# A 3025-point Fourier transform split into 121 by 25 points in place of 55 by 55

## The chip, the core and the metric

The kernel runs on one core of one Trainium2 chip, as one program. The metric is the device time of one execution in microseconds (us), as the median of several runs. The core's engines are TensorE (PE; its weight loads are listed apart as PEld), VectorE (DVE), ScalarE (ACT) and GpSimd (POOL); SyncE (SP) issues most of the transfers.

## The reference

Two layers on a batch of 64 images of 55 x 55 pixels with 96 channels. Layer 0 is a depthwise convolution with 9 x 9 taps, three pixels apart, and a gate. Layer 1 treats the 3025 pixels of an image as tokens: a normalisation, a linear layer to 192 channels with a relu, a Fourier transform along the tokens, a gate on the spectrum, the inverse transform, a linear layer back to 96 channels; then a feed-forward layer with fp8 operands.

```python
def _L1_attn_ref(x, w1, ..., bn2_mean, bn2_var):
    h = jnp.einsum('bnc,hc->bnh', x, w1)
    h = jax.nn.relu(_bn(h, bn1_gamma, bn1_beta, bn1_mean, bn1_var))
    X = jnp.fft.fft(h, axis=1, norm='ortho')
    rd = jnp.diagonal(r)
    idg = jnp.diagonal(i)
    xr = jax.nn.relu(X.real * rd - X.imag * idg + rb)
    xi = jax.nn.relu(X.imag * rd + X.real * idg + ib)
    y = jnp.fft.ifft(xr + 1j * xi, axis=1, norm='ortho').real.astype(jnp.float32)
    o = jnp.einsum('bnh,ch->bnc', y, w2)
    return _bn(o, bn2_gamma, bn2_beta, bn2_mean, bn2_var)

x = _L0_conv_ref(x, L0_conv_raw_kernel, L0_conv_bias)
t = _to_tokens(x)                                  # 64 x 3025 x 96
t = t + _L1_attn_ref(_ln_t(t), ...)
t = t + _L1_ffn_ref(_ln_t(t), L1_ffn_W1, L1_ffn_b1, L1_ffn_W2, L1_ffn_b2)
```

## The kernel before

`conv_stage` computes layer 0 and writes it to `x1` in device memory. `mixer_stage` then sets up constants and runs layer 1, an image (called a batch below) at a time. Its instructions are written out by hand for each engine, in `part(i, ...)`, which `run_all` calls for i = 0 to 66, most of them in a loop. A part works on four batches at once: the forward transform's first half of batch i, its second half, gate, mixing and first inverse half of batch i-1, the last inverse half of batch i-2, and the feed-forward layer of batch i-3. Semaphores tie the engines together.

The transform of 3025 = 55 x 55 points is done in two steps of 55. Tokens lie on 110 partitions, the 55 image rows twice (`NP`), with 28 and 27 token columns side by side (`J` = 28 columns in all, one half padded). The spectrum of a real signal is symmetric, so 28 first frequencies (`K1`) suffice.

A part has two halves.
- First half, loop over h: `turn` transposes the tokens (`tok`), `widen` makes 192 channels of a token column, ACT's `relu` writes `hid`, `rows` is the transform along the partitions (`fa`), DVE's `rows_out` copies it to `arow`, and SP stores that to `a_d`. In between, in eight tiles (`TILE_AT`), `columns` does the second transform of the batch before with weights from `acol`, two tiles of 7 frequencies each at a time in PSUM; ACT's `gate_in`, DVE's `gate` and `join` and POOL gate the spectrum into `spec`. DVE also normalises `xn2` for the feed-forward layer. `acol` is loaded from `a_d`, with the axes exchanged by the address pattern.
- Second half, loop over seven chunks c of four token columns (`JC`): `mix` (two matmuls a frequency, spectrum to 96 channels), `up` (fp8, 384 channels of 440 token slots), `inverse` (second transform backwards, weights from `mixed`), `inverse_rows` (first transform backwards, from `grow`), `down` (fp8, back to 96 channels, weights from `hq`). ACT copies each from PSUM; DVE adds a bias and casts to `hq`, adds the residual into `t2` and takes statistics (`stats`, `variance`) of the coming tokens between the first two chunks; POOL adds the last bias and the output. SP stores `mixed` to `g_d`, loads `grow` from it and `t_res` from `x1`, and stores the output.

`up(c+1)` reuses PSUM that ACT has to empty, and `down(c)` waits for the cast of chunk c (`hq_ready`), so PE, ACT and DVE pass each chunk around.

Of the kernel before, what the change touches and what calls it, by code (L numbers as in the profile page):

```python
# [114 lines left out]


def transform_constants():

    n = np.arange(R)
    k1 = np.arange(K1)  # L120
    ang = 2 * np.pi * np.outer(n, k1) / R
    fwd = np.concatenate([np.cos(ang), -np.sin(ang[:, 1:])], axis=1)
    inv = np.concatenate([np.cos(ang), -np.sin(ang[:, 1:])], axis=1).T
    fa = np.zeros((NP, NP))
    ia = np.zeros((NP, NP))
    for p in range(2):
        fa[p * R:(p + 1) * R, p * R:(p + 1) * R] = fwd
        ia[p * R:(p + 1) * R, p * R:(p + 1) * R] = inv
    k = k1[:, None] + R * n[None, :]
    th = 2 * np.pi * ((n[:, None, None] * k[None]) % (R * R)) / (R * R)  # L130
# [1 line left out]
    fb = np.zeros((NP, K1, NP))
    fb[:R, :, :R] = co
    fb[R:, :, :R] = si
    fb[:R, :, R:] = -si
    fb[R:, :, R:] = co
    w = np.where(k1 == 0, 0.5, 1.0)[None, :, None]
    ib = np.zeros((NP, K1, NP))
    ct, st = (v.transpose(2, 1, 0) * w for v in (co, si))
    ib[:R, :, :R] = ct  # L140
    ib[:R, :, R:] = st
    ib[R:, :, :R] = -st
    ib[R:, :, R:] = ct
    out = {"c_fa": fa, "c_fb": fb, "c_ib": ib, "c_ia": ia, "c_id": np.eye(128)}
# [132 lines left out]
def mixer_stage(nc, x1, p, a_d, g_d, out):  # L277
    with ExitStack() as ctx:
# [22 lines left out]
        b2q = sb("b2q", [NP, C], F16)  # L301


        t_in = sb("t_in", [NP, J, C])
        tok = sb("tok", [NP, J, C + 1])
        xnt = [sb(f"xnt{s}", [C + 1, JC, NP]) for s in range(2)]
        hid = [sb(f"hid{s}", [NP, 2, H]) for s in range(2)]
        arow = [sb(f"arow{s}", [NP, JC, H]) for s in range(AR)]
        acol = sb("acol", [NP, K1, H])
        spec = sb("spec", [HH + 1, 2, K1, NP])  # L310
# [811 lines left out]
```

## Time and profile before

| | us |
|---|---|
| median of 3 runs | 6499.09 |
| lowest, highest | 6497.29, 6509.12 |
| the profiled execution | 6508.48 |
| its span, first to last instruction | 6506.7 |
| PE busy | 5635.0 (87%) |
| DVE busy | 4653.9 (72%) |
| ACT busy | 3317.6 (51%) |
| POOL busy | 2185.0 (34%) |

The convolution takes the first 1050 us or so, the mixer the rest. A table of stretches gives for each the busy time of every engine, the granted TensorE clock (PEclk, 1.00 is full speed), the busy share of the 16 DMA engines and GB/s. A row of a timeline merges like instructions that follow each other: its start, its time to the end of the last, the count as x14, and in brackets the idle time ahead of it with what ended it. An f32 matmul leaves two records, so x14 are 7 matmuls. The end of a matmul is modelled, so its price is read from start to start.

### The profile page before, as it was taken

The numbers are of one execution on the slowest core, as the hardware profiler recorded it, in microseconds if no ns is written. First come the engines' busy times: TensorE is split into PE (matmuls) and PEld (weight loads), VectorE is DVE, ScalarE is ACT, GpSimd is POOL, SyncE is SP. The second block draws the span as 40 slices with busy tenths as digits, with TensorE's granted clock in tenths as the row PEclk, the third lists the DMA queues.
The fourth block names the chain that finished last, engine by engine and source line by source line (L and its number), as shares of the span: only waits on it lengthen the run. The fifth ranks groups of instructions, "written<-read, shape, count | busy, mean of one in ns | idle before, by whom it ended". The sixth has DMA issues, their size and how long they took to land. (4 is left out here: it accounts for less than half of the span.)

```text
span 6506.7 us, 139542 instructions
## 1 busy us (share of the span) xinstructions
PE 5635.0 (87%) x43722; PEld 4751.2 (73%) x43722; DVE 4653.9 (72%) x13238; ACT 3317.6 (51%) x6661; POOL 2185.0 (34%) x1924
## 2 busy tenths in 40 slices
PE   8899994698888888888888888888888888888886
PEld 8898994577777777777777777777777777777775
DVE  4555664367777777777777777777777777777776
ACT  0000000356666666666666666666666666666664
POOL 0000000134444444444444444444444444444443
PEclk9999997789999999999999999999999999999996
DMA  6666664455555555555555555555555555555552
GB/s 219 181 179 189 178 184 113 101 128 132 128 129 129 129 129 128 128 127 128 127 128 128 128 128 128 128 128 128 128 129 129 129 129 128 128 129 129 129 127 60
DMA packets 877318, 875.70 MB, mean 135 GB/s; under 512 B 433439, under 2 KB 805535, under 8 KB 868895
## 3 DMA queue, kind: packets, MB, share of 16 engines
q1 hardware_dynamic: 806005, 784.39, 48.8%
q10 hardware_dynamic: 71174, 89.35, 4.5%
q8 instruction: 100, 1.64, 0.1%
q14 instruction: 39, 0.32, 0.0%
HBM read 497.81 MB, written 375.77 MB: 134 GB/s over the span
## 5 line engine op out<-in xcount | busy, mean ns | idle before, releaser
L646 POOL TENSOR_TENSOR spec<-spec,gc 96x385 f32<-96x385 f32 x512 | 485.7, 949 | 2506.6 <-DVE spec L837 2506.6
L655 POOL TENSOR_TENSOR z<-z,b2q 110x384 f16<-110x384 f16 x448 | 558.7, 1247 | 1622.7 <-ACT z L753 1622.7
L978 PEld LDWEIGHTS ps<-fb,acol 110*96 110x96 f32 (+1 forms) x7168 | 737.9, 164 | 358.9 <-DVE gv L841 230.6
L978 PE MATMUL ps<-fb,acol 110*96 110x110 f32 (+1 forms) x7168 | 817.9, 264 | 122.3 <-DVE gv L841 110.7
L686 ACT ACTIVATE hid<-ps,rstd 110x192 f32<-110x192 f32 x1792 | 660.0, 427 | 487.8 <-PE ps L948 487.2
L958 PE MATMUL ps<-hid,fa 110*110 110x384 f32 x1792 | 754.8, 503 | 165.7 <-ACT hid L686 83.0
L1005 PE MATMUL ps<-w2t,spec 97*110 97x96 f32 x3584 | 742.6, 293 | 13.7 <-DVE spec L848 6.2
L948 PE MATMUL ps<-w1t,xnt 97*110 97x192 f32 x3584 | 734.1, 327 | 0.6 <-ACT xnt L678 0.6
L245 DVE SCALAR_TENSOR_TENSOR xout<-cps,xin 114x351 f32<-114x351 f32 (+3 forms) x512 | 402.4, 786 | 443.4 <-PE cps L272 443.4
L1007 PE MATMUL ps<-w2t,spec 96*110 96x96 f32 x3584 | 718.4, 286 | 0.0
L827 DVE COPY arow<-ps 110x384 f32<-110x384 f32 x896 | 494.6, 552 | 288.0 <-PE ps L958 218.1
L857 DVE TENSOR_TENSOR t<-ps,t_res 110x384 f32<-110x384 f32 x448 | 248.9, 556 | 629.9 <-PE ps L928 488.0
L649 POOL TENSOR_SCALAR gv<-gv 96x385 f32<-96x385 f32 x512 | 657.3, 1284 | 110.7 <-DVE gv L841 110.7
L1064 PEld LDWEIGHTS ps<-w2q,hq 128*110 128x110 fp8e5 x5376 | 397.5, 154 | 406.1 <-issue 378.4
L268 PE MATMUL cps<-xin,toep 114*114 114x117 f32 (+3 forms) x3072 | 615.3, 283 | 87.2 <-DMA xin<-in_x 72.3
L948 PEld LDWEIGHTS ps<-w1t,xnt 97*110 97x110 f32 x3584 | 562.2, 175 | 97.9 <-ACT xnt L678 0.9
L746 ACT ACTIVATE y<-ps 128x1320 f16<-128x1320 f32 x448 | 569.1, 1270 | 106.4 <-PE ps L1048 80.5
L1064 PE MATMUL ps<-w2q,hq 128*110 128x96 fp8e5 x5376 | 415.3, 236 | 233.2 <-issue 225.9
L1005 PEld LDWEIGHTS ps<-w2t,spec 97*110 97x110 f32 x3584 | 583.4, 206 | 35.5 <-issue 29.2
L272 PE MATMUL cps<-xin,toep 114*114 114x96 f32 (+1 forms) x3072 | 570.9, 268 | 0.0
L1007 PEld LDWEIGHTS ps<-w2t,spec 96*110 96x110 f32 x3584 | 569.2, 203 | 0.0
L477 ACT ACT_TABLE_LOAD x1 | 1.3, 1283 | 1079.9 <-PEq L150 1079.9
(103 smaller groups left out, 11789.9 us busy)
## 6 DMA issues: line engine op xcount, KB each, us to landing
a_d<-arow SPq DMA_DIRECT2D x896, 165.0 KB
acol<-a_d SPq DMA_DIRECT2D x64, 1155.0 KB
acol<-a_d SPq DMA_DIRECT2D x64, 1113.8 KB
out<-o_sb SPq DMA_DIRECT2D x832, 82.5 KB
xin<-in_x SPq DMA_DIRECT2D x256, 211.5 KB, 5.4
g_d<-mixed SPq DMA_DIRECT2D x64, 660.0 KB
x_d<-xout ACTq DMA_DIRECT2D x144, 263.2 KB
tok<-x_d SPq DMA_DIRECT2D x64, 577.5 KB
```

The costliest lines, as they stand in the source:

```text
L268: nc.tensor.matmul(o[0:GP, :], toep[0:GP, ch, GP:2 * GP], xs[:, pad:pad + cols], start=True, stop=False)
L272: last = nc.tensor.matmul(o[0:GP, 0:cols - step + pad], toep[0:GP, ch, 0:GP], xs[:, step + pad:], start=False, stop=True)
L649: nc.gpsimd.tensor_scalar(gv[t % 2][:, :, :], gv[t % 2][:, :, :], 0.0, None, ALU.max).then_inc(v_cut, 1)
L655: nc.gpsimd.tensor_tensor(z16[c % 2][:, :, :], z16[c % 2][:, :, :], b2, ALU.add).then_inc(z_biased, 1)
L686: last = nc.scalar.activation(hid[h % 2][:, j, :], ps[0:NP, 5 + h % 2, j * H:(j + 1) * H], ACT.Relu, scale=rstd[0][:, 2 * h + j:2 * h + j ...
L746: nc.scalar.activation(y16[c % 2][:, :, :], ps[:, 4:4 + FM, 0:TOK], ACT.Copy).then_inc(y16_ready, 1)
L948: last = nc.tensor.matmul(ps[0:NP, 5 + h % 2, j * H:(j + 1) * H], xnt[c % 2][:, 2 * (h % 2) + j, :], w1t[:, :], start=True, stop=True)
L958: nc.tensor.matmul(ps[0:NP, 7, 0:2 * H], fa[:, :], hid[h % 2][:, :, :].rearrange("p j h -> p (j h)"), start=True, stop=True).then_inc(a_do ...
L978: last = nc.tensor.matmul(ps[0:HH, 2 - 2 * (t % 2) + n // 4, 128 * (n % 4):128 * (n % 4) + NP], acol[0:kk, k1, hf * HH:(hf + 1) * HH], fb[ ...
L1005: nc.tensor.matmul(o, spec[0:HH + 1, 0, k1, :], w2t[0:HH + 1, 0, :], start=True, stop=False)
L1007: last = nc.tensor.matmul(o, spec[0:HH, 1, k1, :], w2t[0:HH, 1, :], start=False, stop=True)
L1064: last = nc.tensor.matmul(ps[0:NP, 7, C * j:C * (j + 1)], hq[c % 2][:, m, j * NP:(j + 1) * NP], w2q[:, m, :], start=(m == 0), stop=(m == F ...
```

## The change

The tokens now lie on 121 partitions with 25 columns each, which holds 3025 tokens with no padding. The transform is one of 121 points along the partitions and one of 25 along the columns. 61 first frequencies suffice; they are taken in pairs, 31 of them (`PAIRS_K`), each pair with its real and imaginary parts and 25 second frequencies on 100 partitions or columns (`Q`). In `a_d`, `g_d`, `grow` and `arow` the first frequencies are padded to 32 pairs, 128 rows (`M`).

| | before | after |
|---|---|---|
| partitions x token columns | 110 x 28 | 121 x 25 |
| chunks of token columns | 4 x 7 | 4, 4, 4, 4, 3, 3, 3 |
| frequencies in `columns` tiles | 7 x 8 | 8 x 6, 7 x 2 |
| frequencies in `mix` and `inverse` groups | 4 x 7 | 5, 5, 5, 4, 4, 4, 4 |
| size of a `columns` matmul (partitions, weights, moving) | 110, 96, 110 (two of 55) | 100, 96, 100 |
| size of a `mix` matmul | 97 or 96, 110, 96 | 97 or 96, 100, 96 |
| DMAs of a part (`tok`, `t_res`, `grow`, `a_d`, `acol`, `g_d`, `out`) | 2, 2, 4, 14, 2, 2, 14 | 1, 1, 2, 7, 2, 2, 7 |

The load of `acol` now reads runs of 31 x 192 values in two pieces, the store of `arow` writes runs of 192. The unused `t_in` is gone, and with it three memsets of the set-up (`tok`, `t_res`, `grow`); one of 96 values on 100 partitions comes in. The core of the diff:

```diff
-K1 = R // 2 + 1
-J = 28
-NP = 2 * R
+U = 121
+S = 25
+KH = U // 2 + 1
+PAIRS_K = (KH + 1) // 2
+SLOTS = PAIRS_K + 1
+M = 4 * SLOTS
+Q = 4 * S
+CHUNK = (0, 4, 8, 12, 16, 19, 22, 25)
+MIXED = (0, 5, 10, 15, 19, 23, 27, 31)
+GROUP = (0, 8, 16, 24, 31)
+PART = (0, 7, 13, 19, 25)
...
-                nc.vector.memset(tok[:, :, 0:C], 0.0)
-                for v in (t_res, grow):
-                    nc.vector.memset(v[:, :, :], 0.0)
+                nc.vector.memset(mixed[:, PAIRS_K, :], 0.0)
...
-                        for pp in range(2):
-                            sp.dma_start(a_d[i, :, pp * J + JC * c:pp * J + JC * (c + 1), :],
-                                         arow[c % AR][pp * R:(pp + 1) * R, :, :]).then_inc(a_stored[c % AR], 16)
+                        sp.dma_start(a_d[i, c0:c1, :, :].rearrange("s m h -> m s h"),
+                                     arow[c % AR][:, 0:c1 - c0, :]).then_inc(a_stored[c % AR], 16)
...
-                    for ri in range(2):
-                        src = a_d[i, ri * K1:ri * K1 + K1 - ri, 0:R, :].rearrange("k n h -> n k h")
-                        sp.dma_start(acol[ri * R:(ri + 1) * R, ri:K1, :], src).then_inc(acol_in, 16)
+                    src = a_d[i].rearrange("s (r p) h -> (s r) p h", p=SLOTS)
+                    for p0, p1 in ((0, 16), (16, PAIRS_K)):
+                        sp.dma_start(acol[:, p0:p1, :], src[:, p0:p1, :]).then_inc(acol_in, 16)
...
-                    for n in range(KC):
-                        k1 = g * KC + n
-                        kk = R if k1 == 0 else NP
+                    for n in range(pairs):
                         last = nc.tensor.matmul(
-                            ps[0:HH, 2 - 2 * (t % 2) + n // 4, 128 * (n % 4):128 * (n % 4) + NP],
-                            acol[0:kk, k1, hf * HH:(hf + 1) * HH], fb[0:kk, k1, :], start=True, stop=True)
+                            ps[0:HH, 2 - 2 * (t % 2) + n // 4, 128 * (n % 4):128 * (n % 4) + Q],
+                            acol[:, p0 + n, hf * HH:(hf + 1) * HH], fb[:, p0 + n, :], start=True, stop=True)
```

How the order on PE changes at the end of a part's first half, before (`columns` is L978, `widen` L948, `turn` L939, `rows` L958; the numbers are the output's partitions x columns and the count):

```order
L978 MATMUL ps<-fb,acol 96x110 x7
L948 MATMUL ps<-w1t,xnt 110x192 x2
L939 MATMUL ps<-ident,tok 97x110 x4
L958 MATMUL ps<-hid,fa 110x384
L948 MATMUL ps<-w1t,xnt 110x192 x2
L958 MATMUL ps<-hid,fa 110x384
L978 MATMUL ps<-fb,acol 96x110 x7
```

and in the changed kernel (`columns` is L1007, `widen` L978, `turn` L969, `rows` L989):

```order
L1007 MATMUL ps<-fb,acol 96x100 x7
L978 MATMUL ps<-w1t,xnt 121x192 x2
L969 MATMUL ps<-ident,tok 97x121 x3
L989 MATMUL ps<-hid,fa 128x192
L978 MATMUL ps<-w1t,xnt 121x192
L989 MATMUL ps<-hid,fa 128x384
L1007 MATMUL ps<-fb,acol 96x100 x7
```

The order of the groups stays; every second `widen` and `rows` here has one token column in place of two.

The end of a part's second half on PE, before (`up` L1048, `inverse` L1036, `inverse_rows` L928, `down` L1064):

```order
L1048 MATMUL ps<-xq,w1q 128x440 x3
L1036 MATMUL ps<-mixed,ib 110x96 x4
L928 MATMUL ps<-grow,ia 110x384
L1064 MATMUL ps<-w2q,hq 110x96 x12
L1036 MATMUL ps<-mixed,ib 110x96 x4
L928 MATMUL ps<-grow,ia 110x384
L1064 MATMUL ps<-w2q,hq 110x96 x12
L928 MATMUL ps<-grow,ia 110x384 x2
```

and in the changed kernel (L1078, L1065, L958, L1094):

```order
L1078 MATMUL ps<-xq,w1q 128x363 x3
L1065 MATMUL ps<-mixed,ib 100x96 x4
L958 MATMUL ps<-grow,ia 121x384
L1094 MATMUL ps<-w2q,hq 121x96 x9
L1065 MATMUL ps<-mixed,ib 100x96 x4
L958 MATMUL ps<-grow,ia 121x288
L1094 MATMUL ps<-w2q,hq 121x96 x9
L958 MATMUL ps<-grow,ia 121x288 x2
```

Nothing moves here either; the last three chunks have three token columns.

DVE between the first two casts to `hq`, ahead of the second `down`, before:

```order
L901 CAST hq<-y 128x1320
L774 BN_STATS bn<-tok 110x6 x7
L786 TENSOR_TENSOR mean<-bn 110x28
L787 TENSOR_TENSOR diff<-bn 110x28
L788 TENSOR_TENSOR var<-bn 110x28
L789 TENSOR_SCALAR mean<-mean 110x28
L790 SCALAR_TENSOR_TENSOR sq<-diff 110x28
L792 TENSOR_TENSOR var<-var,sq 110x28
L793 TENSOR_SCALAR sq<-var 110x28
L895 TENSOR_SCALAR y<-y,b1q 128x440 x3
L901 CAST hq<-y 128x1320
```

and in the changed kernel:

```order
L930 CAST hq<-y 128x1452
L800 BN_STATS bn<-tok 121x6 x6
L812 TENSOR_TENSOR mean<-bn 121x25
L813 TENSOR_TENSOR diff<-bn 121x25
L814 TENSOR_TENSOR var<-bn 121x25
L815 TENSOR_SCALAR mean<-mean 121x25
L816 SCALAR_TENSOR_TENSOR sq<-diff 121x25
L818 TENSOR_TENSOR var<-var,sq 121x25
L819 TENSOR_SCALAR sq<-var 121x25
L924 TENSOR_SCALAR y<-y,b1q 128x484 x3
L930 CAST hq<-y 128x1452
```

One `bn_stats` less, and adds and casts of 484 slots in place of 440. From the fifth chunk on the cast is `128x3x363`, three rows of 363, since its buffers are 484 wide.

## Rows read from the trace of the kernel before

**Rows 1.** The page's head.

```profile
span 6506.7 us, 139542 instructions
```

**Rows 2.** Timeline of PE: the first `columns` of three batches; start us, us, what.

```profile
1439.86 1.35 PE L978 MATMUL ps<-fb,acol 55*96 55x110 f32 x10
...
1517.69 1.73 PE L978 MATMUL ps<-fb,acol 55*96 55x110 f32 x14
...
5040.47 0.79 PE L978 MATMUL ps<-fb,acol 55*96 55x110 f32 x4
```

**Rows 3.** Timeline of PE: waits ahead of the second and the last `down`.

```profile
1494.10 0.78 PE L1064 MATMUL ps<-w2q,hq 128*110 128x96 fp8e5 x12 [1.81 <-issue]
...
3046.70 1.32 PE L1064 MATMUL ps<-w2q,hq 128*110 128x96 fp8e5 x12 [1.81 <-issue]
...
3071.95 0.78 PE L1064 MATMUL ps<-w2q,hq 128*110 128x96 fp8e5 x12 [1.46 <-issue]
```

**Rows 4.** Stretches: length, busy of PE, PEld, DVE, ACT, POOL; PEclk, DMA share, GB/s.

```profile
1493.00:1498.00 5.00, 3.90 (x41) 3.60 (x42) 2.44 (x6) 2.25 (x5) 1.91 (x2) 1.00 0.78 160
...
3045.00:3050.00 5.00, 3.30 (x24) 3.33 (x25) 3.04 (x8) 1.42 (x4) 1.21 (x2) 0.66 0.78 161
3050.00:3055.00 5.00, 5.00 (x22) 3.75 (x22) 0.00 (x0) 2.25 (x3) 0.61 (x1) 0.50 0.65 156
3055.00:3060.00 5.00, 5.00 (x43) 4.47 (x42) 4.31 (x11) 2.28 (x4) 2.44 (x2) 0.81 0.00 0
```

**Rows 5.** Timeline of PE in the convolution.

```profile
600.50 0.33 PE L270 MATMUL cps<-xin,toep 114*76 114x96 f32 x2
600.67 0.36 PE L272 MATMUL cps<-xin,toep 114*114 114x96 f32 x2
600.87 0.38 PE L268 MATMUL cps<-xin,toep 114*114 114x117 f32 x2
```

**Rows 6.** Timeline of PE: one chunk of the second half.

```profile
3060.52 0.40 PE L1005 MATMUL ps<-w2t,spec 97*110 97x96 f32 x2
...
3062.11 0.72 PE L1048 MATMUL ps<-xq,w1q 96*128 96x440 fp8e5 x3
3062.67 0.92 PE L1036 MATMUL ps<-mixed,ib 110*110 110x96 f32 x8
3063.43 0.82 PE L928 MATMUL ps<-grow,ia 110*110 110x384 f32 x2
3064.09 0.77 PE L1064 MATMUL ps<-w2q,hq 128*110 128x96 fp8e5 x12
3064.69 0.40 PE L1005 MATMUL ps<-w2t,spec 97*110 97x96 f32 x2
```

**Rows 7.** Timeline of PE: groups of the first half, later and first of a batch.

```profile
3009.93 1.49 PE L978 MATMUL ps<-fb,acol 110*96 110x110 f32 x14
3011.26 0.82 PE L948 MATMUL ps<-w1t,xnt 97*110 97x192 f32 x4
3011.91 0.81 PE L958 MATMUL ps<-hid,fa 110*110 110x384 f32 x2
...
3078.42 1.73 PE L978 MATMUL ps<-fb,acol 55*96 55x110 f32 x14
3079.98 0.82 PE L948 MATMUL ps<-w1t,xnt 97*110 97x192 f32 x4
```

**Rows 8.** Timeline of DVE: statistics and casts.

```profile
3041.02 1.21 DVE L774 BATCH_NORM_STATS2 bn<-tok 110x6 f32<-110x96 f32 x7
...
3045.75 0.85 DVE L901 CAST hq<-y 128x1320 fp8e5<-128x1320 f16 x1
...
3070.52 1.33 DVE L901 CAST hq<-y 128x1320 fp8e5<-128x1320 f16 x1
```

**Rows 9.** Groups by form: line, operation, shapes, count | busy us, mean ns | idle before.

```profile
L817 DVE TENSOR_SCALAR xn<-t,mean,rstd 110x96 f32<-110x96 f32 x1792 | 509.1, 368 | 0.1
...
L469 DVE MEMSET grow<- 110x2688 f32 x1 | 2.3, 2298 | 0.5 <-issue 0.5
```

More of the change, by code:

```diff
@@ L110, with half @@
 ROOT_C = 3
-QJ = J // 4
-PAIRS = NC * 2
 TILE_AT = (0, 2, 4, 6, 7, 9, 10, 12)
-TOK = JC * NP
+def half(h):
+    c0, c1 = CHUNK[h // 2], CHUNK[h // 2 + 1]
+    return (c0, c0 + 2) if h % 2 == 0 else (c0 + 2, c1)
 def transform_constants():
[L119 to L130, printed above, removed]
-    co, si = np.cos(th) / R, np.sin(th) / R
[L132 to L144, printed above, removed]
@@ L300, in mixer_stage @@
         b1q = sb("b1q", [128, FM])
[L301 to L310, printed above, removed]
-        gc = [sb(f"gc{s}", [HH, KC, R]) for s in range(2)]
-        gq = [sb(f"gq{s}", [HH, KC, R]) for s in range(2)]
@@ L313, in mixer_stage @@
[L313 to L319 removed]
+        b2q = sb("b2q", [U, C], F16)
+        tok = sb("tok", [U, S, C + 1])
+        xnt = [sb(f"xnt{s}", [C + 1, JC, U]) for s in range(2)]
+        hid = [sb(f"hid{s}", [U, 2, H]) for s in range(2)]
+        arow = [sb(f"arow{s}", [M, JC, H]) for s in range(AR)]
@@ new lines, in mixer_stage @@
+        acol = sb("acol", [Q, PAIRS_K, H])
+        spec = sb("spec", [HH + 1, 2, PAIRS_K, Q])
+        gc = [sb(f"gc{s}", [HH, KC, Q // 2]) for s in range(2)]
+        gq = [sb(f"gq{s}", [HH, KC, Q // 2]) for s in range(2)]
+        gv = [sb(f"gv{s}", [HH, KC, Q // 2]) for s in range(2)]
+        mixed = sb("mixed", [Q, SLOTS, C])
+        grow = sb("grow", [M, S, C])
+        t_res = sb("t_res", [U, S, C])
+        t2 = sb("t2", [U, S, C])
+        xn2 = sb("xn2", [U, S, C])
+        xq = sb("xq", [C, N], F8)
@@ L331, in mixer_stage @@
+        rstd = [sb(f"rstd{s}", [U, S]) for s in range(2)]
         ps = ctx.enter_context(nc.psum_tensor("ps", [128, 8, 512], F32))
@@ L688, in relu @@
+                    act.wait_ge(a_done, i * HALVES + max(h - 1, 0))
+                    s0, s1 = half(h)
+                    for j in range(s1 - s0):
+                        last = nc.scalar.activation(hid[h % 2][:, j, :], ps[0:U, 5 + h % 2, j * H:(j + 1) * H],
+                                                    ACT.Relu, scale=rstd[0][:, s0 + j:s0 + j + 1])
                     last.then_inc(hid_ready, 1)
                 def gate_in(t):
-                    g, hf = t // 2, t % 2
+                    p0, p1, _, hf = group(t)
@@ L709, in part @@
                     turn_out(0)
-                for h in range(PAIRS + 2):
-                    if first and 1 <= h <= PAIRS:
+                for h in range(HALVES + 2):
+                    if first and 1 <= h <= HALVES:
                         relu(h - 1)
```

323 lines of the change are left out of this document (177 added, 146 removed).

## The prediction

> **What bounds the kernel now.** The profiled execution spans 6506.7 us [rows 1] and took 6508.48; the median of the runs shown is 6499.09, 9.4 below it. The convolution stage is not touched, so everything turns on the mixer. Its batches are alike: the first `columns` of the batch starts at 1517.69 and, 43 batches later, at 5040.47 [rows 2], which is 3522.78 / 43 = 81.925 us a batch. 58 batches of the trace have that length.
>
> Read the waits of TensorE (PE) next. PE is busy in almost all of a batch, and its longest waits are two: 1.81 us before the second `down` (it waits for VectorE (DVE), which does statistics and a variance between the two casts `hq`), and 1.46 us before the last `down` [rows 3]. Then read the granted clock. After the 1.81 us wait it is 0.66, 0.50, 0.81 in three stretches of 5 us [rows 4]: full speed is 2.4 GHz, 0.50 is 1.2 GHz, and the three make 2 x 5 x (0.34 + 0.50 + 0.19) = 10.3 us at half speed. This happens once a batch. One batch shows what it costs: in the one before 1517.69 the same wait (1494.10, also 1.81 us) is followed by a clock of 1.00 (the stretch from 1493), and that batch lasts 1517.69 - 1439.86 = 77.83 us [rows 2, 3, 4]. So **a batch is 77.83 us of work and waits, and 4.10 us for one drop of the clock.** After the 1.46 us wait the clock never falls in the batches of that length.
>
> **The price of a matmul.** In the convolution a matmul with 76 weight columns and 96 moving columns takes 0.17 us from start to start, one with 114 weight columns and the same 96 moving takes 0.20 [rows 5]. So the wider of the two sides counts, at (0.20 - 0.17) / (114 - 96) = 0.0017 us a column for f32. fp8 goes at a quarter of that: `down` takes 0.60 for 12 with 110 weight columns, `up` 0.56 for 3 x 440 [rows 6].
>
> **The change part by part, PE work of one batch.**
> - `columns`: 56 matmuls of 110 moving columns at 1.33 / 7 = 0.19 [rows 7] become 62 of 100 at 0.173: 10.64 to 10.73, +0.09. Two of the 56 have only 55 partitions, and their groups take 1.56 in place of 1.33 [rows 7]; no such matmul is left: -0.46. Together -0.37.
> - `mix`: 56 with 110 weight columns at 1.59 / 8 = 0.199 [rows 6] become 62 with 100 at 0.182: 11.14 to 11.28, +0.14.
> - `inverse`: 28 at 0.76 / 4 = 0.19 [rows 6] become 31 at 0.173: +0.04.
> - `widen`: 28 to 25, at 0.65 / 2 each [rows 7]: -0.98.
> - `rows` and `inverse_rows`: 28 token columns to 25, at 0.66 for four in `inverse_rows` [rows 6] and 0.66 for two in `rows`, whose matmul has the same 384 columns: -0.99 and -0.50. Weights of 128 or 121 columns don't count, since 192 or more columns move.
> - `down`: 84 at 0.050 to 75 at 0.055: -0.10. `up`: 3080 token slots to 3025: -0.07. Transposes: 56 x 110 columns to 50 x 121, nothing.
>
> The sum is **-2.8 us of PE work a batch**. The padding goes (110 x 28 = 3080 slots for 3025 tokens, now 121 x 25 = 3025), and the price of 31 pairs against 28 is nearly paid by their being 100 wide and not 110.
>
> **What of it lies on the path.** PE waits for other engines between its work, so the -2.8 counts only if their chains shrink too. DVE loses 3 of 28 normalisations at 509.1 / 1792 = 0.28 us each (0.85) [rows 9] and 6 of 56 statistics at 1.21 / 7 = 0.17 (1.04) [rows 8], -1.9, and the copies and residual adds of three token columns; the gates keep their size (28 x 55 = 1540 to 31 x 50 = 1550 elements). ScalarE (ACT) loses 3 of 28 relus. Where the work sits matters: the chunks are now 4, 4, 4, 4, 3, 3, 3, and the mixing groups 5, 5, 5, 4, 4, 4, 4. So the early part of the second half of a batch gets heavier, and the end much lighter.
> - Ahead of the second `down`, PE has 10 matmuls of `mix` for 8 (+0.23), 5 of `inverse` for 4 (+0.105), 484 slots in `up` for 440 (+0.06) and 121 columns in `down` (+0.055): +0.45. The DVE chain it waits for does 6 statistics for 7 (-0.17), and its adds and its cast grow by a tenth (0.85 to 0.93, and the adds likewise): about 0. So the +0.45 is hidden, and the wait shrinks from 1.81 to about **1.4 us**.
> - Ahead of the last `down`, PE has 0.34 less (`down` -0.11, `inverse` -0.07, `inverse_rows` -0.16), DVE's cast goes from 1.33 [rows 8] to 1.33 x 1089 / 1320 = 1.10 and its adds by as much in proportion, -0.37: the wait stays 1.4.
>
> The PE sum counts the hidden +0.45 as a price, so on the path it would be -3.2; against that, other waits grow where a chain on DVE or ACT shrinks less than PE's work. I let the two cancel. I take **-2.8**, with ends of -1.9 (what two DVE groups lose, if DVE set the pace everywhere) and -3.5 (the PE sum with the +0.45 hidden, and a little of the last wait). A batch without a drop is then 77.83 - 2.8 = **75.0 us** (74.3 to 75.9).
>
> **The clock.** Both long waits are then 1.4 us, and the rows have a wait of 1.46 us after which it never fell and one of 1.81 us after which it mostly did. So I take it that the drop goes: another 4.1 us. That is more than all the work saved, and the least certain term.
>
> **Transfers.** The loads of `acol` become contiguous (31 pairs of 768 B on 100 partitions), but the stores of `arow` become what these loads were: 768 B pieces, 3200 a batch. It moves the short pieces and does not remove them. Neither is on the path: the queues are empty in the stretch that begins at 3055 (a DMA share of 0.00) [rows 4], 19 us before the next batch (24 x 81.925 before 5040.47, at 3074) needs `acol`. The loads of `tok` and `grow` keep their 384 B pieces. I count 0, and 0 to both sides, since that cover is 19 us.
>
> **Fill and drain.** Some 7.5 batches' worth of work stand outside the 58: 7.5 x 2.8 = -21. Of the setup three memsets of 2.3 us go [rows 9]: -7. Sum -28.
>
> **The sum**, against the profiled execution: 58 x (81.925 - 75.0) = -402, and -28: 6508.5 - 430 = 6079. The median lies 9.4 lower: **6070 us**. With the ends of the batch, 6020 to 6120.
>
> **Rivals.**
> - *The drop stays* in each batch, or moves to the last `down`. For it: a wait of 1.4 is nearer to 1.46 than to 1.81, but my two estimates may be off by 0.2 each, and the work between 1.46 and 1.81 is not seen. 58 x 2.83 = -164, -28: 6316, median **6307**. The drop at the end has a mechanism of its own: the casts of 3 token columns are no longer one run but three rows of 363. If the second half of the elements goes on a second port by rows, two rows stand against one. Were the cast so bound, 1.33 would become 1.33 x 1452 / 1320 = 1.46 and not 1.10, and the wait 1.8. The Trainium skill, "Vector Engine (DVE) Microarchitecture Reference", section 5.1, says just this: with two ports "the first port takes the larger half of an odd outermost count". No row of the trace has such a shape; by that rule this rival is the likely one, but the same form takes 0.85 and 1.33 [rows 8], so in the late chunks something else than the ports binds it. Chance of the rival 0.20.
> - *The drop stays in a part of the batches*, as it is missing in one now: half of them gives 6188. Chance 0.14.
> - *Slower: two drops a batch*, the old one (the wait stays at 1.6 or more) and one at the last `down` (its wait passes the same point). It decides between 1.46 and 1.81 us at both places. 75.0 + 2 x 4.1 = 83.2 us, 58 x 1.27 = +74, -28: median **6545**. Chance 0.04.
> - *The change only pads differently and the waits take the saving back*, with the drop in place: between 6310 and 6545, about no change. Widths of 121 leave fp8 operands on odd bytes, which no row shows. Chance 0.04.
> - Better than 6010: 0.03.
>
> **How the numbers follow.** The forecast (6020 to 6120) has 0.55. The range reaches from 6010 to 6310, so that it takes in the half-way case and most of the first rival: about 0.82. Faster by over 0.2% (13 us; about what a measurement of this kernel can tell) 0.92, within it 0.03, slower 0.05.
>
> **What the profile after would show.** From `columns` to `columns` 75.0 us, with 78 to 79 if the drop stays; a granted clock of 1.00 in the middle of the mixer; waits near 1.4 us before the second and the last `down`; `columns` groups of 8 in 1.38 us and 7 in 1.21, and `mix` groups of 10 in 1.8; the first `columns` group of a batch no longer slower than the others. It is wrong if `mix` and `inverse` keep 0.19 us a matmul (+1.6 us a batch), if casts of 363 take as long as those of 484, or if the clock still falls.

## The result, and the profile after

| | before | after |
|---|---|---|
| median of 4 runs each, us | 6498.19 | 6216.35 |
| lowest, highest | 6496.06, 6509.12 | 6204.41, 6237.3 |
| ratio, 95% interval | | 0.9572, 0.9544 to 0.960 |
| the profiled execution, its span | 6508.48, 6506.7 | 6218.28, 6216.1 |
| mean granted clock | 0.92 | 0.95 |
| PE busy in the span | 5635.0 | 5297.6 |

The change saves 282 us, where some 430 were forecast (6070). The time lies in the range (6010 to 6310) and on the right side, but outside the forecast (6020 to 6120), and a third of the expected gain is missing.

The stretches of the profile after come first. A fall is a stretch in which the granted clock is at half speed, what the prediction calls a drop; the steady batches are the 58 alike ones in the middle. Columns: length, then busy time of PE, PEld, DVE, ACT, POOL, then the granted clock, the DMA share and GB/s. The first row is 58 batches in steady state; then one batch without a fall of the clock and one with two; then six stretches around the places where it falls.

```profile
1414.08:5902.84 4488.76, 3868.31 (x31787) 3233.84 (x31785) 3542.52 (x10499) 2937.48 (x5858) 1766.08 (x1740) 0.98 0.56 139
...
2584.78:2660.59 75.81, 65.03 (x551) 54.20 (x549) 61.03 (x182) 50.60 (x101) 30.29 (x30) 1.00 0.57 142
3045.27:3123.83 78.56, 68.09 (x551) 57.06 (x549) 61.07 (x182) 50.72 (x101) 30.53 (x30) 0.96 0.55 137
3000.00:3005.00 5.00, 2.96 (x17) 1.83 (x16) 3.70 (x9) 3.78 (x9) 2.83 (x4) 1.00 0.73 136
3005.00:3010.00 5.00, 5.00 (x34) 4.62 (x34) 1.08 (x5) 1.60 (x4) 0.67 (x1) 0.66 0.74 181
3021.00:3026.00 5.00, 4.77 (x52) 4.23 (x53) 1.92 (x6) 2.99 (x6) 1.94 (x2) 1.00 0.63 182
3038.00:3043.00 5.00, 2.81 (x30) 2.25 (x29) 4.67 (x14) 1.37 (x4) 1.49 (x2) 0.98 0.38 104
3043.00:3048.00 5.00, 5.00 (x31) 4.47 (x30) 3.43 (x18) 0.82 (x3) 1.46 (x2) 0.68 0.31 91
3048.00:3053.00 5.00, 5.00 (x38) 4.29 (x37) 2.20 (x5) 5.00 (x13) 0.96 (x1) 1.00 1.25 200
```

A batch takes 4488.76 / 58 = 77.39 us on average, against 81.925 [rows 2]; 58 x 4.53 = 263, and the span fell by 290.6. One without a fall takes 75.81; the one before took 77.83. The clock still falls, in two new places: at the end of the first half of a batch (3005 to 3010: 0.66) and after the last `down` (3043 to 3048: 0.68). Such a fall lasts some 2 x 5 x 0.34 = 3.4 us at half speed, a third of the 10.3 of before. Where the fall of before was, after the second `down` (3021 to 3026), the clock is 1.00 [rows 4]. In the 58 batches the record of the clock has 23 falls of the first kind and 39 of the second; 19 of the batches have neither, but all but two of these begin with the end of a fall of the batch before; the batch with both costs 78.56 - 75.81 = 2.75 us more than the one that no fall touches.

The waits of PE in the timeline around these places: the end of the first half, the second `down` and the last `down`. Between them stand two ordinary groups, each from its first row to the start of the row shown behind it: `mix` of 10 matmuls (3012.30 to 3014.07) and `columns` of 8 (3049.51 to 3050.88).

```profile
3003.16 0.59 PE L989 MATMUL ps<-hid,fa 121*128 121x192 f32 x2 [1.18 <-ACT hid L707]
...
3012.30 0.34 PE L1034 MATMUL ps<-w2t,spec 97*100 97x96 f32 x2
...
3014.07 0.78 PE L1078 MATMUL ps<-xq,w1q 96*128 96x484 fp8e5 x3
...
3021.23 0.84 PE L1094 MATMUL ps<-w2q,hq 128*121 128x96 fp8e5 x12 [1.15 <-issue]
...
3042.09 0.68 PE L1094 MATMUL ps<-w2q,hq 128*121 128x96 fp8e5 x9 [2.19 <-issue]
...
3049.51 1.54 PE L1007 MATMUL ps<-fb,acol 100*96 100x100 f32 x16
3050.88 0.83 PE L978 MATMUL ps<-w1t,xnt 97*121 97x192 f32 x4
```

The wait at the end of the first half is 1.18, and the kernel before had one of 1.32 there, with no fall behind it:

```profile
3029.78 0.90 PE L958 MATMUL ps<-hid,fa 110*110 110x384 f32 x2 [1.32 <-ACT hid L686]
```

The wait before the second `down` is 1.15 (1.81 before), the one before the last is 2.19 (1.46 before) [rows 3]. That last one was forecast at 1.4. What PE waits for there is DVE; this is DVE's and then POOL's timeline ahead of 3042.09:

```profile
3038.66 0.73 DVE L800 BATCH_NORM_STATS2 bn<-t 121x6 f32<-121x96 f32 x4
3039.31 1.63 DVE L924 TENSOR_SCALAR y<-y,b1q 128x363 f16<-128x363 f16 x3
3041.07 0.92 DVE L930 CAST hq<-y 128x1089 fp8e5<-128x1089 f16 x1
```

```profile
3039.17 0.73 POOL L675 TENSOR_TENSOR z<-z,b2q 121x288 f16<-121x288 f16 x1 [1.39 <-ACT z L779]
3040.06 0.76 POOL L678 TENSOR_TENSOR o_sb<-t,z 121x288 f32<-121x288 f32 x1 [0.17 <-POOL z L675]
```

Three bias adds take 1.63 us, with POOL at work in the same 1.6 us: the first of the three takes 0.70, the second 0.30, the third 0.78, and the first and the third each started while a POOL instruction was running. Over the whole trace an add of 363 elements takes 0.305 us when POOL is idle or starts after it (all but one of 271). 305 others started inside a POOL instruction, and all but one of these end 0.11 to 0.12 us after it, so that most last 0.70 to 0.97 us, and 0.34 those 51 for which POOL was nearly through. An add of 484 elements takes 0.34 and 0.84. POOL starts at 3039.17, DVE at 3039.31: POOL is first by 0.14 us. These rows gave the first theory.

### The profile page after: what moved, and what is told of

It is laid out like the page before. It is cut to its first block and busy times, and to the rows that moved or that the text cites. A ratio compares the mean times of both kernels' runs of the same rounds, so it can differ in the third digit from the quotient of the medians.

```text
span 6216.1 us, 136648 instructions
## 1 busy us (share of the span) xinstructions
PE 5297.6 (85%) x44298; PEld 4566.4 (73%) x44298; DVE 4527.8 (73%) x12660; ACT 3248.1 (52%) x6469; POOL 1951.5 (31%) x1924
## 3 DMA queue, kind: packets, MB, share of 16 engines
q8 instruction: 100, 1.64, 0.1%
## 5 line engine op out<-in xcount | busy, mean ns | idle before, releaser
L1007 PEld LDWEIGHTS ps<-fb,acol 100*96 100x96 f32 x7936 | 778.8, 170 | 316.0 <-DVE gv L868 233.7
L1007 PE MATMUL ps<-fb,acol 100*96 100x100 f32 x7936 | 815.4, 257 | 124.2 <-DVE gv L868 116.2
L989 PE MATMUL ps<-hid,fa 121*128 121x384 f32 (+1 forms) x1792 | 708.6, 477 | 187.5 <-DVE arow L854 106.7
L707 ACT ACTIVATE hid<-ps,rstd 121x192 f32<-121x192 f32 x1600 | 602.7, 432 | 482.8 <-PE ps L978 482.6
L1034 PE MATMUL ps<-w2t,spec 97*100 97x96 f32 x3968 | 718.2, 264 | 19.1 <-DVE spec L875 19.1
L1036 PE MATMUL ps<-w2t,spec 96*100 96x96 f32 x3968 | 702.3, 260 | 0.0
L667 POOL TENSOR_SCALAR gv<-gv 96x400 f32<-96x400 f32 (+1 forms) x512 | 663.9, 1297 | 106.4 <-DVE gv L868 106.3
L978 PE MATMUL ps<-w1t,xnt 97*121 97x192 f32 x3200 | 680.7, 330 | 0.7 <-ACT xnt L698 0.7
L1094 PEld LDWEIGHTS ps<-w2q,hq 128*121 128x121 fp8e5 x4800 | 326.5, 139 | 420.3 <-issue 394.7
L771 ACT ACTIVATE y<-ps 128x1452 f16<-128x1452 f32 (+1 forms) x448 | 561.0, 1252 | 56.2 <-PE ps L1078 43.1
L1094 PE MATMUL ps<-w2q,hq 128*121 128x96 fp8e5 x4800 | 350.0, 222 | 269.3 <-issue 263.7
L1034 PEld LDWEIGHTS ps<-w2t,spec 97*100 97x100 f32 x3968 | 544.3, 176 | 39.6 <-issue 29.3
L978 PEld LDWEIGHTS ps<-w1t,xnt 97*121 97x121 f32 x3200 | 514.7, 185 | 55.4 <-ACT xnt L698 1.0
L1036 PEld LDWEIGHTS ps<-w2t,spec 96*100 96x100 f32 x3968 | 537.2, 176 | 0.0
```

Source lines behind the costliest of these rows:

```text
L667: nc.gpsimd.tensor_scalar(gate_buffer(gv, t), gate_buffer(gv, t), 0.0, None, ALU.max).then_inc(v_cut, 1)
L707: last = nc.scalar.activation(hid[h % 2][:, j, :], ps[0:U, 5 + h % 2, j * H:(j + 1) * H], ACT.Relu, scale=rstd[0][:, s0 + j:s0 + j + 1])
L771: nc.scalar.activation(y16[c % 2][:, :, 0:n], ps[:, 4:4 + FM, 0:n], ACT.Copy).then_inc(y16_ready, 1)
L978: last = nc.tensor.matmul(ps[0:U, 5 + h % 2, j * H:(j + 1) * H], xnt[c % 2][:, 2 * (h % 2) + j, :], w1t[:, :], start=True, stop=True)
L989: nc.tensor.matmul(ps[0:M, 7, 0:n * H], fa[:, :], hid[h % 2][:, 0:n, :].rearrange("p j h -> p (j h)"), start=True, stop=True).then_inc(a_d ...
L1007: last = nc.tensor.matmul(ps[0:HH, 2 - 2 * (t % 2) + n // 4, 128 * (n % 4):128 * (n % 4) + Q], acol[:, p0 + n, hf * HH:(hf + 1) * HH], fb[ ...
```

## The experiments

### What makes the wait before the last `down`

**Experiment 1** holds POOL back until VectorE is through.

```diff
                         pool.wait_ge(z_ready, b * NC + c + 1)
+                        pool.wait_ge(hq_ready, b * NC + min(c + 2, NC))
+                        pool.sem_inc(pool_passed, 1)
```

> The changed kernel, with POOL's two operations on chunk c (add of the last bias, output) held until VectorE has cast chunk c+1. Nothing is left out. Theory A: the wait of 2.19 us before the last `down` is that long because POOL's add starts 0.14 us ahead of VectorE's three bias adds of 363 and holds them up (1.63 us where three adds of 0.305 take 0.95). Then here the last three adds take 0.95 us, the wait falls from 2.19 to 1.5, a batch without a drop from 75.81 to 75.1, and the clock no longer falls after that wait: about 6216 - 58 x (0.7 + 0.8) = 6130 us. Theory B: adds of 363 elements are slow in themselves: they keep 1.2 to 1.6 us for three, the wait stays above 2, the time within 15 us of 6216.

Measured: 6013.93 us, ratio 0.9249 (0.9229 to 0.9268). DVE and then PE at the end of a batch without a fall:

```profile
1770.46 0.75 DVE L926 TENSOR_SCALAR y<-y,b1q 128x363 f16<-128x363 f16 x3
1771.35 0.92 DVE L932 CAST hq<-y 128x1089 fp8e5<-128x1089 f16 x1
```

```profile
1772.37 0.68 PE L1096 MATMUL ps<-w2q,hq 128*121 128x96 fp8e5 x9 [1.32 <-issue]
```

The adds take 0.75 (less than the 0.95 said, as one starts 0.22 us after the other), so the width of 363 was not what made them slow: theory B is out. The wait is 1.32 and the clock never falls after it; the 23 falls at the end of the first half stay. The gain is much larger than the 86 us expected, 202 us, since a batch without a fall takes 73.83 and not 75.1: the wait of 1.15 before the *second* `down` went too. POOL had held up VectorE there as well. In the changed kernel, DVE and then POOL ahead of 3021.23:

```profile
3017.60 0.78 DVE L818 TENSOR_TENSOR var<-var,sq 121x25 f32<-121x25 f32 x1
3018.42 0.18 DVE L819 TENSOR_SCALAR sq<-var 121x25 f32<-121x25 f32 x1
3018.72 1.35 DVE L924 TENSOR_SCALAR y<-y,b1q 128x484 f16<-128x484 f16 x3
```

```profile
3017.39 0.95 POOL L675 TENSOR_TENSOR z<-z,b2q 121x384 f16<-121x384 f16 x1 [11.72 <-ACT z L779]
3018.50 0.91 POOL L678 TENSOR_TENSOR o_sb<-t,z 121x384 f32<-121x384 f32 x1 [0.17 <-POOL z L675]
```

L818 takes 0.19 where POOL is idle, and three such adds 0.86: 0.6 and 0.5 us together are about the 1.15.

**Experiment 2** lays the three-column chunks in one run for the cast.

```diff
+        def packed(buf, c):
+            w = (CHUNK[c + 1] - CHUNK[c]) * U
+            w += w % 2
...
-                        nc.vector.tensor_copy(hq[c % 2][:, :, 0:n], y16[c % 2][:, :, 0:n],
+                        w = FM * yv.shape[2]
+                        nc.vector.tensor_copy(flat(hq, c)[:, 0:w], flat(y16, c)[:, 0:w],
```

> The changed kernel, with the feed-forward buffers of the three-column chunks laid out 364 apart and not 484, so that the cast to `hq` is one run of 1092 elements and not three rows of 363. Nothing is left out. Theory A: the three rows are split as two against one, so that 726 elements set the time; one run of 1092 halves evenly: the cast goes from 0.918 to 0.918 x 0.5 x 1092 / 726 and a fixed part, about 0.73 us; the last wait from 2.19 to 2.0, the time by 58 x 0.19 = 11 us or less, 6205. Theory B: the odd width of 363 costs: then too 0.73, but the bias adds, which keep that width, stay as they are. Theory C: neither, a fixed time for the cast: 0.92 stays and 6216.

Measured: 6163.65 us, ratio 0.9472 (0.9446 to 0.9499).

```profile
3329.58 1.63 DVE L933 TENSOR_SCALAR y<-y,b1q 128x363 f16<-128x363 f16 x3
3331.34 0.73 DVE L940 CAST hq<-y 128x1092 fp8e5<-128x1092 f16 x1
```

The cast takes 0.73 for three more elements than the 0.92 of three rows, the adds stay, and the wait is 2.00: as theories A and B both say, so this run alone does not part them. Other rows speak for A. Casts in one run take 0.73 for 1092 elements, 0.85 for 1320 and 0.92 for 1452, which is about 0.00105 us for each element of a half; three rows of 363, split as two against one, have 726 in the larger part, just as 1452 has in a half, and take 0.92 as well. And the odd width costs the adds nothing: 0.30 for 363, 0.34 for 484. The time fell by more than the 11 us expected, 53 us: the wait of 0.60 before the fifth `down` shrank too (0.41), so a batch without a fall takes 75.44 (-0.37, 21 us), and there are 37 falls in the 58 batches in place of 62. Why these went, no run isolates.

**Experiment 3** gives VectorE another order, and leaves POOL alone.

```diff
-                        if c > LAG:
+                        if c > LAG and not (third and c < NC):
                             residual_stats(c - LAG - 1)
...
                                               saturate=False).then_inc(hq_ready, 1)
+                        if prep and c > LAG:
+                            residual_stats(c - LAG - 1)
```

> The changed kernel, with VectorE's residual statistics of a chunk (0.73 us) moved behind the bias adds and the cast of the coming chunk; they stood ahead of them. Nothing is left out. Theory A (the last `down` waits for VectorE's own order): the last adds start 0.65 us earlier, which is before POOL's add, so they take 0.95 and not 1.63; the wait falls from 2.19 to about 0.8, a batch without a drop from 75.81 to about 74.5, and the drop after it goes: 6216 - 58 x (1.3 + 0.8) = about 6095 us. Theory B (the statistics only change place and the end of the batch waits for them): the wait goes but what follows takes it back, 6216 - 58 x 0.8 = 6170, the clock alone.

Measured: 6071.96 us, ratio 0.934 (0.9318 to 0.9361). DVE and POOL ahead of the last `down`:

```profile
1483.04 0.76 DVE L924 TENSOR_SCALAR y<-y,b1q 128x363 f16<-128x363 f16 x3
1483.94 1.22 DVE L930 CAST hq<-y 128x1089 fp8e5<-128x1089 f16 x1
```

```profile
1483.55 0.83 POOL L675 TENSOR_TENSOR z<-z,b2q 121x288 f16<-121x288 f16 x1 [1.42 <-ACT z L779]
```

Now the adds are first and take 0.76, and the cast, begun at 1483.94 while POOL works until 1484.38, takes 1.22 in place of 0.92: the delay moved on to the next VectorE instruction and shrank. The wait is 0.98 (0.8 said), the batch without a fall 74.62 (74.5), and no fall is left after the last `down`: theory A. A fall stands at the end of the first half in 43 of the 58 batches (75.23 and not 74.62 us, so these cost 0.6 each): more than the 23 of the changed kernel, at the same wait (1.19).

**Experiment 8** makes the edit of the first experiment in the kernel before.

> The kernel before, with the same edit as the first experiment: POOL's work on chunk c is held until the cast of chunk c+1. Nothing is left out. In the kernel before POOL held up the late casts (1.33 in place of 0.85 us). Theory A (the contention was there before as well, the change only moved it from the casts to the adds and made it dearer): the late casts fall to 0.85, the wait before the last `down` from 1.46 to about 1.0, the wait of 1.81 and the drop after it stay: 81.92 - 0.5 to 1.0 a batch, 6440 to 6470 us. Theory B (the change brought the contention): within 10 us of the kernel before.

Measured: 6270.35 us, ratio 0.963 (0.9579 to 0.968). A batch without a fall takes 75.38, 2.4 less than the 77.83 of before. The wait before the last `down` is 0.98, as theory A says (1.0), but the 1.81 us wait, which was expected to stay, is 0.60, and the time is 170 us below the expected range:

```profile
1722.64 0.78 PE L1066 MATMUL ps<-w2q,hq 128*110 128x96 fp8e5 x12 [0.60 <-issue]
```

The rows say why: DVE and POOL in the kernel before, ahead of its second `down`,

```profile
3042.74 0.80 DVE L789 TENSOR_SCALAR mean<-mean 110x28 f32<-110x28 f32 x1
...
3043.89 0.78 DVE L793 TENSOR_SCALAR sq<-var 110x28 f32<-110x28 f32 x1
```

```profile
3042.60 0.91 POOL L655 TENSOR_TENSOR z<-z,b2q 110x384 f16<-110x384 f16 x1 [10.38 <-ACT z L753]
3043.67 0.96 POOL L659 TENSOR_TENSOR o_sb<-t,z 110x384 f32<-110x384 f32 x1 [0.17 <-POOL z L655]
```

and the same two instructions with POOL held:

```profile
1719.90 0.18 DVE L791 TENSOR_SCALAR mean<-mean 110x28 f32<-110x28 f32 x1
...
1720.42 0.18 DVE L795 TENSOR_SCALAR sq<-var 110x28 f32<-110x28 f32 x1
```

Two instructions on 28 elements took 0.80 and 0.78 us and not 0.18, each ending 0.04 us after POOL's did: 1.22 us together, which is the 1.81 less the 0.60. So the wait ahead of the fall in the kernel before was for two thirds VectorE waiting for POOL.

In both kernels and in experiments 1, 3 and 8 the rule is the same: of an add, a cast or one of these small operations and a POOL instruction, whichever starts first goes on at full speed, and the other waits for its end. The time for which it waits is part of its row. Not every VectorE operation is held: in experiment 1 `bn_stats` takes 0.24 us with a POOL instruction at work that was there first (1769.80 to 1770.53), as it does without one. The Trainium skill, "SBUF — State Buffer", section "SBUF: two separate sides", says this: the port pair that VectorE and GpSimd share is an exclusive lock held for the whole instruction. The traces agree (0.18 against 0.80, 0.305 against up to 0.97 us). That POOL's work is held up in turn was seen too. In the kernel before, DVE and then POOL ahead of the last `down`:

```profile
3069.58 0.80 DVE L895 TENSOR_SCALAR y<-y,b1q 128x440 f16<-128x440 f16 x3
```

```profile
3069.63 1.52 POOL L655 TENSOR_TENSOR z<-z,b2q 110x384 f16<-110x384 f16 x1 [1.17 <-ACT z L753]
```

The adds are first by 0.05 us and keep their 0.80; POOL's `z` takes 1.52 where 0.91 is usual, and the cast that starts while it runs takes the 1.33 of [rows 8].

### What the falls of the clock cost

**Experiment 4** fills the two waits with matmuls whose output nobody reads.

```diff
+                def fill(n, bank):
+                    for _ in range(n):
+                        nc.tensor.matmul(ps[0:U, bank, 0:28], ia[:, :], ident[:, 0:28],
+                                         start=True, stop=True)
...
+                        if h == HALVES + 1:
+                            fill(4, 5)
                         rows(h - 2)
...
+                        if c == NC:
+                            fill(8, 0)
                         down(c - 1)
```

> The changed kernel with matmuls that nobody reads in the two stretches after which the clock falls: eight of 121 weight columns and 28 moving columns ahead of the last `down`, four ahead of the last `rows`, about 0.2 us each, inside waits of 2.19 and 1.18 us. The result is the same. It prices the clock alone. Theory A (idle TensorE ahead of it makes the clock fall): both waits end when they did, the clock stays 1.00, every batch takes 75.8 us: 6216 - 58 x 1.6 = 6125 us. Theory B (the falls have another cause, such as the power of all engines together): the clock falls as before or more, 6216 or above.

Measured: 6175.21 us, ratio 0.9491 (0.9468 to 0.9515). All 23 falls at the end of the first half went, of the 39 after the last `down` 26 stayed (the text of experiment 9 says 25), so theory A held in part (6125 was expected), and theory B is out. Batches without a fall take 75.84, as expected, so the filling itself costs nothing. **Experiment 9** widens the moving side of the filling to 128.

> As the fourth experiment, but the twelve matmuls that nobody reads move 128 columns each and not 28; with 121 weight columns they should take about as long, 0.2 us. In the fourth the falls ahead of the second half went (23 of 23), of the 39 after the last `down` 25 stayed. Theory A (short moving sides leave TensorE too idle there): the rest go as well, all batches take 75.8 us: 6216 - 58 x 1.6 = 6125 us. Theory B (the stretch after the wait, or something else than TensorE's work, decides): about 25 falls stay, about 6175.

Measured: 6130.61 us, ratio 0.9424 (0.94 to 0.9449), and not one fall in the steady batches. Thirty of them in a row:

```profile
2629.87:4906.26 2276.39, 2029.70 (x17162) 1713.70 (x17161) 1833.35 (x5431) 1520.39 (x3030) 912.74 (x900) 1.00 0.57 142
```

That is 75.88 us a batch. Theory A of that run came true (6125). The falls cost the changed kernel 6216 - 6131 = 86 us (by the two ratios to the kernel before, 96).

**Experiment 12** does this in the kernel before (seven of 128 ahead of the second `down`, five ahead of the last, four ahead of the last `rows`).

> The kernel before with matmuls of 128 moving columns that nobody reads inside its three long waits: seven ahead of the second `down` (1.81 us), five ahead of the last (1.46), four ahead of the last `rows` (1.32). Nothing is left out. With the ninth run it shows both kernels without a fall of the clock. Theory A (the prediction's reading: 77.83 us of work and waits and 4.10 for the fall): every batch takes 77.8, 6500 - 58 x 4.1 = 6262 us. Theory B (the one batch read there, which has a wait of 0.60 us before the fifth `down`, is 0.9 us longer than one in step; in the sixth run a batch without a fall took 76.55, and 76.95 with the 0.40 back): 6500 - 58 x 4.97 = 6212 us. Theory C (falls of the clock have another cause): about 6500.

Measured: 6259.03 us, ratio 0.9615 (0.9599 to 0.9631); again thirty batches:

```profile
2678.77:5004.22 2325.45, 2131.60 (x17132) 1750.94 (x17131) 1891.02 (x5701) 1551.83 (x3120) 980.47 (x900) 1.00 0.56 136
```

77.52 us a batch: theory A (6262), and B and C are out. So the falls cost the kernel before 6507 - 6259 = 248 us, and reading 77.83 + 4.10 from one batch was right within 0.3. The two kernels without falls in their steady batches differ by 0.9424 / 0.9615 = 0.980, 2.0% or 128 us; the other 2.3%, about 160 us, is the clock. In the steady batches the falls cost 81.92 - 77.52 = 4.40 us before and 77.39 - 75.88 = 1.51 after, so 2.89 of the 4.53 us that a batch lost are the clock's. **More than half of what the change brings it brings through the clock.**

**Experiment 5** takes the wait of the kernel before away in another manner.

```diff
-                    if more and c < 4 - EARLY:
-                        n = EARLY + c
+                    if more and c == 1:
+                        n = EARLY
```

> The kernel before, with the last statistics of the coming tokens and their variance (some 3.7 us of VectorE, rows 8 and what follows) moved from between the first two casts to behind the second. Nothing is left out. It prices the clock's drop in the kernel before. Theory A: the wait of 1.81 us before the second `down` goes, the clock stays 1.00 there, a batch falls from 81.92 to between 76.0 (drop and wait both gone) and 77.8 (the drop alone): 6500 - 58 x (4.1 to 5.9) = 6160 to 6260 us. Theory B: the wait moves to the third `down`, and the drop with it: 6450 to 6510.

Measured: 6279.59 us, ratio 0.9632 (0.9583 to 0.9682). The wait is gone (0.49 is left, before the third `down`), a batch without a fall takes 75.73, and no fall stands at the old place. The time misses the expected range by 20 us, since a new kind came: in 10 batches the clock falls 39 us into the batch, at the end of the first half, and stays low for 30.7 us. Such a batch takes 87.95. Eight others have a fall of 3.4 us there. Experiment 8 has 12 of the long ones and 3 of the short; one of the long in two stretches:

```profile
2274.85:2309.85 35.00, 32.07 (x217) 25.55 (x216) 31.92 (x93) 27.48 (x64) 16.61 (x16) 1.00 0.52 136
2309.85:2349.85 40.00, 37.30 (x221) 32.17 (x221) 19.96 (x71) 18.55 (x32) 8.14 (x9) 0.62 0.49 105
```

It is why these two gained less than their batches without a fall promise: 58 x (81.92 - 75.73) = 359 us here and 58 x (81.92 - 75.38) = 379 in experiment 8, where 226 and 236 were measured; 10 and 12 long falls at 12.1 to 12.2 us each are 122 and 145.

### Where the saved work went

**Experiment 6** pads the two half-high matmuls of the kernel before.

```diff
-                        kk = R if k1 == 0 else NP
+                        kk = NP
```

> The kernel before, with the two matmuls of 55 partitions in `columns` made over all 110 (the other 55 hold zeros, one memset in the set-up): the group of 7 that held one took 1.56 us against 1.33. Nothing is left out. Theory A (the prediction): both groups take 1.33, and 0.46 us a batch less work on TensorE shortens the path: 58 x 0.46 = 27 us, 6475. Theory B: the work goes (1.33 us a group), but the next wait for VectorE's gate, 22.52 us into the batch in both kernels, takes it back: within 5 us of the kernel before.

Measured: 6423.76 us, ratio 0.9863 (0.9843 to 0.9884). The first `columns` group takes 1.33:

```profile
4421.65 1.49 PE L979 MATMUL ps<-fb,acol 110*96 110x110 f32 x14
4422.98 0.82 PE L949 MATMUL ps<-w1t,xnt 97*110 97x192 f32 x4
```

and all that follows in the first half comes 0.40 us earlier (the wait of `rows` ends at +13.36 and not +13.77, the transposes for the feed-forward start at +38.99 and not +39.39). Theory B is out: nothing takes it back. But 0.40 x 58 is 23 us, and 82 were saved, which neither theory foretold. The fall of 10.2 us, which stood in every steady batch of the kernel before but one, now stands in 32 of 58; six have one of 6.8 at that place, one has 30.7, and 37 have one of 3.4 at the end of the first half, many of them besides the long one. Together the clock is low for 526 us of the 58 batches and not for 594. At the 0.4 us for each us at half speed that falls cost elsewhere, these 68 us would be an estimated 27 to 29. That leaves about 30 of the 82 that nothing here accounts for; no run isolates it.

**Experiment 7** takes VectorE work out of the first half of the changed kernel. It leaves out 18 of 25 normalisations of a batch, so its output is not the model's; it only asks for a time.

```diff
-                    for j in range(CHUNK[c], CHUNK[c + 1]):
+                    for j in range(CHUNK[c], CHUNK[c + 1] if isinstance(i, int) and i < 4 else CHUNK[c] + 1):
```

> The changed kernel, where VectorE normalises one token column of each chunk for the feed-forward layer and leaves out the other 18 of 25 (the old values stay in place), from the fifth part on: 18 x 0.31 = 5.6 us less of VectorE in the first half of a batch. It asks whether VectorE or TensorE sets the pace there. Theory A (VectorE does, which is why 0.4 us of the work saved there turned into waits): the waits of `rows` for the copies (1.03, 0.21, 0.43 us) and of `columns` for the gate (three of 0.59) shrink, a batch falls by 1 to 3 us, 6216 - 58 x 2 = 6100. Theory B (TensorE's own order does): within 15 us of 6216.

Measured: 6101.87 us, ratio 0.9376 (0.936 to 0.9393). A batch without a fall takes 74.61. The wait of `rows` for the copies, first in the changed kernel, then here:

```profile
2598.41 0.56 PE L989 MATMUL ps<-hid,fa 121*128 121x384 f32 x1 [1.03 <-DVE arow L854]
```

```profile
2783.11 0.56 PE L989 MATMUL ps<-hid,fa 121*128 121x384 f32 x1 [0.30 <-DVE arow L854]
```

Of 5.6 us less on VectorE 1.2 came through, most of it in two of the seven waits of that half (1.03 to 0.30 and 0.59 to 0.35); the other waits stayed. The 114 us saved are more than 58 x 1.2 = 70, since the falls changed as well: 16 are left at the end of the first half and 23 after the last `down`, ten of these 6.8 us long. VectorE sets the pace in a part of the first half, and the pairs of `rows` and copy (0.21, 0.43) and `columns` and gate (0.59) wait for each other whatever VectorE does besides.

### A faster kernel

**Experiment 10** has the edits of experiments 1, 2 and 3 together.

> The changed kernel with three edits of experiments 1 to 3 together: POOL held until the next cast, the late casts as one run of 1092, the residual statistics behind the cast. Theory A (their savings on the wait before the last `down` add, as they stand one behind the other in VectorE's chain): the wait of 1.32 of the first experiment falls by 0.19 and 0.65 to about 0.5, a batch without a fall from 73.83 to 72.9; the falls at the end of the first half stay and cost about 0.2 on average: 6014 - 58 x 0.9 = 5962 us. Theory B (held POOL work comes out of the way too late for the residual, or TensorE's own work is next): 73.8 stays, 6010.

Measured: 5966.2 us, ratio 0.918 (0.9155 to 0.9204). A batch without a fall takes 72.50 (72.9 expected), with a wait of 0.77 before the last `down` where theory A said 0.5; 27 of the 58 batches have a fall at the end of the first half and take 72.9 to 73.6. **Experiment 11** adds the filling there.

> The three edits and four matmuls of 128 moving columns that nobody reads ahead of the last `rows`, inside the wait of 1.18 us. Theory A: no fall of the clock is left in the steady batches, granted clock 1.00, each batch as long as the shortest of the run before, about 72.9: 5950 us. Theory B: the matmuls cost more than the falls they spare (0.6 us each at about 2 batches in 5): 5965 or more.

Measured: 5918.46 us, ratio 0.9096 (0.9072 to 0.9119). All steady batches take about 72.5 us:

```profile
1563.51:1636.04 72.53, 65.73 (x558) 55.29 (x557) 60.02 (x182) 50.63 (x101) 29.89 (x31) 1.00 0.60 149
...
1634.08 0.68 PE L1115 MATMUL ps<-w2q,hq 128*121 128x96 fp8e5 x9 [0.77 <-issue]
```

Nothing of the computation is left out, and it is faster than both kernels: by 9.0% than the one before and, set against the changed kernel's 0.9572, by 5.0% than that. The filling was expected to bring 12 us and brought 48 between the medians; between the two profiled executions it is 28, of which 58 x 0.31 = 18 lie in the steady batches (72.83 to 72.52 on average) and the rest outside them.

## Why the prediction was right and wrong

The change was rightly seen to save both work and falls of the clock, and the time lies in the range. But the forecast proper (6020 to 6120, given 0.55) missed; the range held because it had been drawn wide enough for a rival. Two of its own signs of being wrong came true: the clock still falls, and casts of 363 take as long as those of 484.

- **Price of the matmuls, right.** A `columns` group of 8 takes 3050.88 - 3049.51 = 1.37 us (1.38 said); `mix` of 10 takes 1.77 (1.8). PE's busy time in a batch without a fall goes from 67.56 to 65.03: -2.53 (-2.8 said). The 0.46 for two half-high matmuls is 0.40 in experiment 6.
- **What of it lies on the path, wrong by 0.8 us a batch.** "I let the two cancel" was the step. A batch without a fall went down by 2.02 and not by 2.8: 0.27 is the work, 0.51 are waits (10.27 to 10.78 us a batch). In the first half PE's busy time falls by 1.97, the half by 1.56 (39.39 to 37.83), since `rows` now waits for VectorE's copies twice more (0.21, 0.43). Over thirty batches with the waits filled it is 77.52 to 75.88, -1.64. The lower end of the stated bounds, 1.9, was nearer.
- **The wait before the second `down`, right number, wrong reason.** 1.4 said, 1.15 measured. I costed VectorE's chain by its own work. Two thirds of the old wait were POOL's hold on it (experiment 8) and nearly all of the new one (experiment 1), and a POOL operation that starts a little earlier or later changes what is held up.
- **The wait before the last `down`, wrong.** 1.4 said, 2.19 measured, and here the forecast of the clock fell too. "Its adds by as much in proportion" was the step. The adds went from 0.80 to 1.63 because POOL's `z` now came 0.14 us ahead of them; in the kernel before it came 0.05 us behind, and the cast was held up (1.33, where the same form takes 0.85). Both rows stood in the trace; I took 1.33 as a price of the cast. Lengths of VectorE beside a busy POOL can't be scaled by elements.
- **The cast of three rows.** 1.10 said; 0.92 measured, what POOL doesn't hold. The rule of the Trainium skill ("Vector Engine (DVE) Microarchitecture Reference", section 5.1) that the first port takes the larger half of an odd outermost count fits the rows: three rows of 363 cost what one run of 1452 costs, both with 726 elements in the larger part, and one run of 1092 costs 0.73 (experiment 2). That rival's outcome (the fall moves to the last `down`) came in 39 of 58 batches, but the adds brought it, not the cast.
- **"So I take it that the drop goes", half right.** It went from its place, where the wait shrank, and came back in two others: 62 falls of 3.4 us in 58 batches. Of 248 us of falls 163 went. What I had was one wait with a fall and one without; the falls at the end of the first half, behind a wait of 1.18 with one of 0.43 ahead and 0.42 behind, I did not look for, though the kernel before has 1.32 us there. The case nearest to what came is the rival "in a part of the batches", given 0.14 and 6188 us; it meant the old fall in half of the batches, and not short new ones at two places, so that its time is near (28 us) is luck in part.
- **Transfers, fill and drain, right.** No wait of PE in the batch ends with a transfer. 290.6 - 263 = 28 us lie outside the 58 batches, as said; no run tests its two parts.
- **The sum.** 430 us said against 290 between the two profiled executions: 58 x 0.81 = 47 us for the path and 58 x (77.39 - 75.81) = 92 us for the falls that stay make the 139 that are missing.

## What to carry to other kernels

Read every VectorE duration beside what GpSimd does in that moment: two lengths of one form (0.85 and 1.33, 0.18 and 0.80) are a sign of one engine holding up the other, and the cure is to hold GpSimd's slack work until VectorE's urgent chain is through, here 202 us for one semaphore wait. Ask of TensorE's waits not only how long they are but whether the clock falls behind them, and price this apart, by filling the waits with matmuls that nobody reads. A gain counted in work alone can be half of the story or twice it.
